# Recurrent stage: squares of the Newton chain on ScalarE, a later row transpose, the last deviations as columns

## The reference

```python
def _L1_ffn_ref(x, ln_w, ln_b, W, b):
    def step(h, _):
        h = h + 0.01 * jnp.tanh(h)
        h = h * jax.nn.sigmoid(h)
        h = _layernorm(h, ln_w, ln_b)
        h = jnp.einsum('bsc,dc->bsd', h, W) + b
        return (h, None)
    x, _ = jax.lax.scan(step, x, None, length=30)
    return x
...
x = x + _L1_ffn_ref(_layernorm(x, axis=-1), ln_w, ln_b, W, b)
```

## Time and profile before

| | us |
|---|---|
| median of 3 runs | 3229.25 (3229.11 to 3229.91) |
| profiled execution, its time | 3229.77 |
| its span, first to last instruction | 3228.0 |
| mean granted TensorE clock | 0.977 of full speed |
| busy: PE, DVE, ACT, POOL | 3034.4, 2831.7, 2382.6, 1722.1 |

### The profile page before, as it was taken

The page is one execution under the profiler, slowest core; times in us unless marked ns, Lnnn a source line. Parts: engine busy times, 40 slices in busy tenths (PEclk is TensorE's granted clock), DMA queues, the critical chain, the costliest instruction groups (busy, mean ns, idle before and its releaser), DMA issues. The chain is left out here.

```text
span 3228.0 us, 67245 instructions
## 1 busy us (share of the span) xinstructions
PE 3034.4 (94%) x16801; PEld 2092.0 (65%) x16801; DVE 2831.7 (88%) x8856; ACT 2382.6 (74%) x4988; POOL 1722.1 (53%) x1101
## 2 busy tenths in 40 slices
PE   6999896999999899999999489999999999999997
PEld 4666665888888577777777355555555555555556
DVE  4777776888888788888888779999999999999997
ACT  4666664444444577777777699999999999999993
POOL 2444444333332121211211058899898888888886
PEclk9999997999999999999999589999999999999999
DMA  4000000000000000000000035555555555555557
GB/s 130 17 19 16 16 16 14 1 0 0 0 0 0 25 14 10 13 12 11 13 10 4 3 132 195 198 184 188 198 190 184 197 195 184 190 199 188 187 197 245
DMA packets 135071, 290.03 MB, mean 90 GB/s; under 512 B 12081, under 2 KB 69601, under 8 KB 135009
## 3 DMA queue, kind: packets, MB, share of 16 engines
q1 hardware_dynamic: 118112, 280.89, 25.7%
q10 hardware_dynamic: 16896, 8.39, 0.9%
HBM read 278.88 MB, written 10.35 MB: 90 GB/s over the span
## 5 line engine op out<-in xcount | busy, mean ns | idle before, releaser
L1077 POOL TENSOR_TENSOR d_g<-d_g,d_rb 128x1024 f32<-128x1024 f32 x480 | 1121.1, 2371 | 269.6 <-DMA d_rb<-d_rstd_rows 269.6
L1265 PE MATMUL d_p_y<-d_g,d_w_main 128*128 128x512 f32 x1856 | 960.9, 599 | 0.0
L1279 PEld LDWEIGHTS d_p_gt<-ident,d_g 128*128 128x128 f32 x3840 | 466.0, 142 | 527.7 <-ACT d_g L1324 365.1
L1142 DVE BATCH_NORM_STATS2 d_stats<-d_p_gt 128x6 f32<-128x256 f32 x1920 | 712.7, 407 | 24.1 <-PE d_p_gt L1279 24.1
L1324 ACT ACTIVATE d_g<-d_th,d_bias 128x512 f32<-128x512 f32 x928 | 670.2, 722 | 67.1 <-DVE d_th L1135 37.3
L1135 DVE SCALAR_TENSOR_TENSOR d_th<-d_th,d_p_y 128x512 f32<-128x512 f32 x960 | 638.0, 665 | 4.4 <-ACT d_th L1320 4.3
L1320 ACT ACTIVATE d_th<-d_p_y,d_bias 128x512 f32<-128x512 f32 x928 | 621.7, 670 | 1.3 <-PE d_p_y L1265 1.2
L1279 PE MATMUL d_p_gt<-ident,d_g 128*128 128x128 f32 x3840 | 592.0, 277 | 0.0
L514 ACT ACTIVATE a_prob<-a_masked,a_neg_max 128x128 f32<-128x128 f32 x1024 | 327.4, 391 | 111.5 <-DVE a_neg_max L334 111.4
L434 PE MATMUL a_p_s<-a_k_heads,a_q_t 128*128 128x512 f32 x768 | 397.4, 599 | 0.5 <-DVE a_k_heads L310 0.5
L451 PEld LDWEIGHTS a_p_pv<-a_v_ones,a_prob_t 128*128 128x128 f32 x3072 | 373.7, 192 | 10.7 <-issue 10.3
(11 more groups left out here) (170 smaller groups left out, 4399.5 us busy)
## 6 DMA issues: line engine op xcount, KB each, us to landing
d_rb<-d_rstd_rows SPq DMA_DIRECT2D x480, 512.0 KB, 5.5
a_adj_in<-in_adj_dram SPq DMA_DIRECT2D x64, 256.0 KB, 2.8
out_dram<-d_out_sb ACTq DMA_DIRECT2D x32, 256.0 KB, 3.3
d_rstd_rows<-d_rstd_row SPq DMA_DIRECT2D x120, 16.0 KB, 1.4
m_w_sb<-in_L_ffn_w_dram SPq DMA_DIRECT2D x2, 512.0 KB
x_sb<-in_x_dram SPq DMA_DIRECT2D x1, 256.0 KB, 2.9
a_w_raw<-in_L_gnn_Wq_dram SPq DMA_DIRECT2D x2, 64.0 KB, 2.1
a_w_raw<-in_L_gnn_Wk_dram SPq DMA_DIRECT2D x2, 64.0 KB, 2.1
```

The lines of the kernel that those rows point to most:

```text
L1077: nc.gpsimd.tensor_tensor(g[:, c, :], g[:, c, :], rb[:, buf, :], ALU.mult).then_inc(s_gs, 1)
L1142: ins = nc.vector.bn_stats(stats[:, q % 2, (j * CT + t) // 2].rearrange("p a s -> p (a s)"), p_gt[:, t * P:(t + 2) * P].rearrange("p (a c) ...
L1265: nc.tensor.matmul(p_y[:, c % 2, cols(u)], w_main[:], g[:, c, cols(u)], start=True, stop=True).then_inc(s_y, 1)
L1279: ins = nc.tensor.transpose(p_gt[:, t * P:(t + 1) * P], g[:, c, t * P:(t + 1) * P], ident[:])
```

## The change: what it does, and the diff

The chain is written so that three of its steps are squares: y^2 after the guess, (v y^2 - 5/3)^2, and (3/8 y)^2. ScalarE makes them (newton_square, with its own places); VectorE keeps six instructions. The chain has 9 steps and ends at the same place as before (r = 3, place 0). The factor -1/2 goes into the weights.

rstd becomes one buffer for each of the four groups, so the guess waits for the row transpose of four groups before. The row transpose moves behind the transposes of unit 0 in slot c mod 4 = 2.

The last four groups' deviations are not transposed, stored, spread and multiplied into g. The last product waits for silu alone, and add_x multiplies by the deviation as a column: four instructions of 128x128 for one of 128x512. It waits for the chain and for s_xb. OUTS becomes 8. Row transposes, copies, SP's loop and GpSimd's loop run over 116 groups (SPREADS) in place of 120. GpSimd's waits for the whole normalised x and for the preparation move ahead of its first multiplication. The preparation has one step more, a memset, and TensorE and ScalarE wait for it.

```diff
-    CHAIN, XCHAIN, PLACES = 10, 12, 3
+    SPREADS = ALL_GROUPS - GROUPS
+    CHAIN, XCHAIN, PREP = 9, 12, 11
-    RSTD_SCALE = 3.0 / 8.0
-    OUTS = 4
+    PLACES = {(0, 0): 0, (0, 1): 1, (1, 0): 3, (1, 2): 5, (2, 2): 7, (3, 0): 8}
+    ACT_PLACES = {(0, 1): 2, (1, 0): 4, (2, 0): 6}
+    CUBIC, SQUARE = 3.0 / 8.0, -1.0 / 2.0
+    OUTS = 8
...
-        rstd = sb("rstd", [P, GTILES])
-        vy2 = sb("vy2", [P, GTILES])
+        rstd = sb("rstd", [P, GROUPS, GTILES])
+        y2 = sb("y2", [P, GTILES])
+        centre = sb("centre", [P, 1])
...
-        v, work, v_x, work_x = (p_nw[:, n * GTILES:(n + 1) * GTILES] for n in range(4))
+        v, vy2, off, v_x, work_x = (p_nw[:, n * GTILES:(n + 1) * GTILES] for n in range(5))
...
# GpSimd
+                pool.wait_ge(s_xn, CHUNKS * UNITS)
+                pool.wait_ge(s_prep, PREP)
                 with pool.Fori(1, CHUNKS + 1) as i:
                     for c in range(CHUNKS):
                         scale(i, c)
-                    pool.wait_ge(s_prep, 10)
-                    pool.wait_ge(s_xn, CHUNKS * UNITS)
...
-                with pool.Fori(CHUNKS + 1, ITERS + 1) as i:
+                with pool.Fori(CHUNKS + 1, ITERS) as i:
...
# VectorE, newton(k, q, n)
-                    y = rstd[:]
+                    y = rstd[:, q, :]
...
-                            wait(dve, s_rt, k)
+                            wait(dve, s_rt, k - GROUPS + 1)
                             ins = nc.vector.tensor_scalar(y.bitcast(I32), v.bitcast(I32), -0.5, MAGIC, ALU.mult, ALU.add)
-                        elif n == 2 or n == 7:
-                            ins = nc.vector.tensor_tensor(work, v, y, ALU.mult)
-                        elif n == 3:
-                            ins = nc.vector.tensor_tensor(vy2[:], work, y, ALU.mult)
-                        elif n == 4:
-                            ins = nc.vector.scalar_tensor_tensor(out=work, in0=vy2[:], scalar=-10.0 / 3.0, in1=work,
+                        elif n == 3 or n == 7:
+                            ins = nc.vector.tensor_tensor(vy2, v, y2[:], ALU.mult)
+                        elif n == 5:
+                            ins = nc.vector.scalar_tensor_tensor(out=y, in0=off, scalar=20.0 / 9.0, in1=y,
                                                                  op0=ALU.add, op1=ALU.mult)
-                        elif n == 5:
-                            ins = nc.vector.tensor_tensor(work, work, y, ALU.mult)
-                        elif n == 8:
-                            ins = nc.vector.scalar_tensor_tensor(out=work, in0=work, scalar=-0.5 * RSTD_SCALE ** 2, in1=y,
-                                                                 op0=ALU.mult, op1=ALU.mult)
                         else:
-                            ins = nc.vector.scalar_tensor_tensor(out=y, in0=work, scalar=5.0 if n == 6 else 1.5, in1=y,
+                            ins = nc.vector.scalar_tensor_tensor(out=y, in0=vy2, scalar=-3.0, in1=y,
                                                                  op0=ALU.add, op1=ALU.mult)
...
# VectorE, add_x(o, u)
+                    n, q = o * UNITS + u, o // GC
                     dve.wait_ge(s_y, units(SLOTS + o, u))
+                    dve.wait_ge(s_nw, CHAIN * (ALL_GROUPS - GROUPS + q + 1))
+                    dve.wait_ge(s_xb, CHUNKS)
                     wait(dve, s_out[n % OUTS], 16 * (n // OUTS))
-                    nc.vector.tensor_tensor(out_sb[:, n % OUTS].rearrange("p (t c) -> p t c", t=UT),
-                                            p_y[:, o % 2, cols(u)].rearrange("p (t c) -> p t c", t=UT),
-                                            x_sb[:, tile:tile + UT, :], ALU.add).then_inc(s_sum, 1)
+                    for t in range(UT):
+                        tile = u * UT + t
+                        ins = nc.vector.scalar_tensor_tensor(
+                            out=out_sb[:, n % OUTS, t * P:(t + 1) * P], in0=p_y[:, o % 2, tile * P:(tile + 1) * P],
+                            scalar=rstd[:, q, o % GC * CT + tile:o % GC * CT + tile + 1], in1=x_sb[:, o * CT + tile, :],
+                            op0=ALU.mult, op1=ALU.add)
+                    ins.then_inc(s_sum, 1)
...
# TensorE, last_product and the row transpose
-                    pe.wait_ge(s_gs, s - CHUNKS + 1)
+                    pe.wait_ge(s_g, units(s - CHUNKS, u))
...
                             if live(s - 2):
                                 transpose_g(s - 2, (c - 2) % CHUNKS, u)
-                        k = GROUPS * i + (c - 9) // GC
-                        if c % GC == 1 and live_group(k):
-                            transpose_rstd(k)
+                            k, q = GROUPS * i + (c - 10) // GC, (c - 10) // GC % GROUPS
+                            if c % GC == 2 and u == 0 and spread_group(k):
+                                transpose_rstd(k, q)
...
# ScalarE
+                def newton_square(k, q, n):
+                    act.wait_ge(s_nw, CHAIN * k + n)
+                    if n == 4:
+                        ins = nc.scalar.activation(off, vy2, ACT.Square, bias=centre[:])
+                    else:
+                        ins = nc.scalar.activation(y2[:], rstd[:, q, :], ACT.Square, scale=1.0 if n == 2 else CUBIC)
+                    ins.then_inc(s_nw, 1)
...
                             nc.scalar.copy(rstd_row[:, q % 2, :], p_rt).then_inc(s_row, 1)
+                        newton_part(i, c, 0)
                         if live(s):
                             tanh(s, c % 2, 1, col)
                             silu(s, c, 0, col)
+                        newton_part(i, c, 1)
...
-                act.wait_ge(s_prep, 7)
+                act.wait_ge(s_prep, PREP)
```

More of the change, by code:

```diff
@@ L1027, in live_group, with spread_group @@
             return not isinstance(k, int) or 0 <= k < ALL_GROUPS
+        def spread_group(k):
+            return not isinstance(k, int) or 0 <= k < SPREADS
         def iterations(eng, body):
@@ L1032, in iterations @@
             body(1)
-            with eng.Fori(2, ITERS) as i:
+            with eng.Fori(2, ITERS - 1) as i:
                 body(i)
+            body(ITERS - 1)
             body(ITERS)
@@ L1062, in _ @@
                 body(0)
-                with sp.Fori(1, ITERS) as i:
+                with sp.Fori(1, ITERS - 1) as i:
                     body(i)
                 for par in range(2):
-                    sp.wait_ge(s_dw[par], 16 * ALL_GROUPS // 2)
+                    sp.wait_ge(s_dw[par], 16 * SPREADS // 2)
                     for j in range(GC):
-                        sp.wait_ge(s_rb[par * GC + j], 16 * ALL_GROUPS // 2)
+                        sp.wait_ge(s_rb[par * GC + j], 16 * SPREADS // 2)
             @block.gpsimd
@@ L1178, in newton_part @@
                     k, q = GROUPS * i + (c - 6) // GC, (c - 6) // GC % GROUPS
[L1179 to L1180 removed]
+                    n = PLACES.get(((c - 6) % GC, place))
+                    if n is not None and live_group(k):
                         newton(k, q, n)
                 def add_x(o, u):
[L1184 removed]
+                    n, q = o * UNITS + u, o // GC
                     dve.wait_ge(s_y, units(SLOTS + o, u))
+                    dve.wait_ge(s_nw, CHAIN * (ALL_GROUPS - GROUPS + q + 1))
+                    dve.wait_ge(s_xb, CHUNKS)
                     wait(dve, s_out[n % OUTS], 16 * (n // OUTS))
[L1187 to L1190 removed]
+                    for t in range(UT):
[5 more added lines that the diff above has]
+                    ins.then_inc(s_sum, 1)
                 def body(i):
@@ L1211, in body @@
                             if c in (0, 1, 4, 5, 8, 9):
-                                for n in range(c % GC * 6, c % GC * 6 + 6):
+                                for n in range(c % GC * 6, min(c % GC * 6 + 6, XCHAIN)):
                                     newton_of_x(1 + c // GC, n)
@@ L1220, in _ @@
                     stats_of_x(GC + c)
-                    for n in range(3 * c, 3 * c + 3):
+                    for n in range(3 * c, min(3 * c + 3, XCHAIN)):
                         newton_of_x(0, n)
@@ L1236, in _ @@
                 link(nc.vector.tensor_copy(bias_bc[:], p_gt[:, P:2 * P]))
+                link(nc.vector.memset(centre[:], -5.0 / 3.0))
                 iterations(dve, body)
-                dve.wait_ge(s_xb, CHUNKS)
                 add_x(CHUNKS - 1, 1)
@@ L1280, in transpose_g, with transpose_rstd @@
                     ins.then_inc(s_gt, 1)
-                def transpose_rstd(k):
+                def transpose_rstd(k, q):
                     pe.wait_ge(s_nw, CHAIN * (k + 1))
                     wait(pe, s_row, k)
-                    nc.tensor.transpose(p_rt, rstd[:], ident[:]).then_inc(s_rt, 1)
+                    nc.tensor.transpose(p_rt, rstd[:, q, :], ident[:]).then_inc(s_rt, 1)
                 def body(i):
@@ L1324, in silu, with newton_part @@
                     nc.scalar.activation(g[:, c, cols(u)], th[:, c % 2, cols(u)], ACT.Silu, bias=col).then_inc(s_g, 1)
+                def newton_square(k, q, n):
```

(8 more changed lines are left out.)

8 lines of the change are left out of this document (2 added, 6 removed).

## The result

| | us |
|---|---|
| before, median | 3229.58 |
| changed kernel, median of 4 runs | 3175.3 (3173.52 to 3179.61) |
| ratio, 95% interval | 0.9836 (0.9821 to 0.9851) |
| changed kernel, profiled execution: its time, its span | 3179.61, 3177.7 |

The change takes 54 us off by the medians; the forecast was 3184 with 3170 to 3207 as range.

What follows compares the result with a forecast made beforehand. The prediction took VectorE, 99.9% busy at 11.07 us a group, as the bound. Its terms gave 3229.8 - 40.1 (chain) + 1.9 (start) - 7 (end) = 3184.6 us, against the median 3184, range 3170 to 3207.

Steps and rivals of the forecast that it cites:

- What bounds the kernel: Iterations 1 to 29 of the recurrent stage: VectorE, 99.9% busy, sets the pace at 11.07 us a group.
- The chain: Recurrent groups: six of ten steps stay on VectorE, three squares go to ScalarE; period 11.07 to 10.72 us, gain 40 us.
- Do the squares make anybody wait: Squares on ScalarE in the recurrent groups: no wait of VectorE on them, the tightest having 0.3 us to spare.
- The row transpose: TensorE, one unit later: its 43.5 us of waits for the chain end, but are worth nothing in time.
- The start: Preparation and iteration 0: memset and waits 0.3 us, eight squares 1.0, GpSimd's later start 0.6; sum +1.9 us.
- The end: Last four groups, without spreads and GpSimd multiplications, with eight output buffers: -7 us, bounds -10 and 0.
- A: Recurrent groups: VectorE, ScalarE and TensorE rub, period 10.80 to 11.0 us, total 3194 to 3216; chance 0.17.
- B: Recurrent groups: ScalarE becomes the bound at 11.41 us with squares of 0.40 us, total about 3263; chance 0.05.
- C: ScalarE: Square shares no table with Tanh and Silu, two loads per square, total some 4150 us; chance 0.03.
- D: Recurrent groups: VectorE alone sets the pace, steps worth more, 10.62 us a group, frictionless end, 3169 to 3176; chance 0.07.
- the forecast's own range: Whole kernel: 3176 to 3196 us, from a period of 10.67 to 10.80 and an end of -3 to -10; chance 0.66.

Runs made afterwards that it cites:

- the version at 10.592: Changed kernel with a chain of eight steps, five on VectorE, epsilon added in two other steps, GpSimd's waits at their old place: 3166.73 us, ratio 0.9806.

## Why the prediction was right, and where its terms were off

**What bounds the kernel.** Right. VectorE was the bound and is the bound; each step on it is worth 0.10 us a group, shown by taking four away (10.673), one more away (10.592, 0.09 us) and adding one (10.775).

**The chain.** Right in direction and in VectorE's 10.67 us; the term was 40 us and measured 45.0. The step that failed is the price of the squares: "Sum 0.48 us, and ScalarE goes to 10.70 us". I took start-to-start distances of small copies and added them, which is right for small instructions in a row; between large activations the neighbours give part of it back, and ScalarE stands at 10.39. So there was no tie between two engines at 10.7, and the 0.05 us a group that I put on top of VectorE's 10.67, 5 of the 115 groups' 45 us, had no cause. The estimate from the Trainium skill, page "ScalarE: Activation LUTs" (ScalarE at 10.67), erred in the same way. The weakness of it was the row: small copies behind one another, and none between large activations.

**Do the squares make anybody wait.** Right: no wait of VectorE for ScalarE in 1230 us.

**The row transpose.** Right that it is worth nothing, by an experiment; also the wait would have gone without it.

**The start.** +1.9 forecast, +3.1 measured. The late start of GpSimd and the clock that came back later make 2.3 us of it, where I had put 0.6: GpSimd's first multiplication began at 1893.67, when the last normalise had ended at 1893.4, and the first product waited 0.69 us for it and then ran at the 1.2 GHz level. Moving the waits back took the 2.3 us off; but the run with four output buffers is rid of 1.9 of them with the late waits in place and the clock back early. So I had left out the clock at the seam between iterations 0 and 1, which has its own price; whether the late waits keep it down isn't shown. The 1.0 us for eight squares was too much, 0.3 to 0.7 by the traces with early waits.

**The end.** -7 forecast, -10.1 measured. My ideal sum, 36.2 us of VectorE's work, was what it took (36.0); "with 2 us for two resources so nearly equal" was the mis-sized part. VectorE at 1.00 did not wait for the DMA engines at 0.87 (3160 to 3165 us). Of the remaining 1.1 us, 0.5 is the last store (2.8 us from the last sum's end to the span's and not 3.3), and 0.4 lies ahead of the first sum, where the chain is shorter. I had counted the gain for the spreads and multiplications that go; but with four output buffers it would have been 1.9 us smaller.

**The rivals.** A (the engines rub) is refuted down to 0.01 us a group, even in the version at 10.592, where TensorE needs 10.49. B needed 0.28 us a square; it is 0.04 to 0.12, and even eight more a group cost only 35 us. C: no table load but the one of the earlier trace rows. D, that VectorE alone sets the pace, is what happened, with the end without friction; its time, 3169 to 3176, holds the measured 3175.3, though not for its reason, that the steps are worth more (10.62 us a group; it was 10.678). I had given it 0.07. So the forecast's own range, 3176 to 3196, was missed by 0.7 us, and the full range held.

**How much was luck.** Between the profiled executions the forecast's 3184.6 is 5.0 us above the 3179.61. Its errors of 4.9 us on the chain and 3.1 on the end have the same sign; the start, 1.2 us the other way, and the stages ahead, which ran 1.75 us longer, took 3 us off them by chance. Against the median 3184 is 8.7 us off.

**The rule** of the Trainium skill, page "ScalarE: Activation LUTs", rules for kernel authors, that multiplications belong on VectorE, would have been the costly way here. The trace disagrees with it as a matter of time: the chain with three steps on ScalarE takes 43 us off (3227.42 to 3184.44), for VectorE is the bound and ScalarE has room. The 9.8% of the run with the squares on VectorE are another matter: four steps with both inputs in SBUF beside a busy GpSimd, one of them no square. That is a price which the prediction missed altogether. Each step of the old chain that takes two tiles has one of them in PSUM, and a square of a tile in SBUF has not. By the count alone three steps would have cost 34 us, an estimate from the price of one step.

**What stays open.** Why a tanh behind a square takes 0.57 us to the next start and behind a silu 0.63 is not explained, only measured. A version with the squares on VectorE and their inputs in PSUM was not tried, so the 34 us are argued, and it isn't shown that nine steps need ScalarE. How the start's cost divides between GpSimd's late waits and the clock is open, too.

## What to carry to other kernels

Where one engine is busy all the time, count its instructions by start-to-start distance, and trust the sum; here engines at 97 to 99% of the bound did not add anything. Before an elementwise step is put on VectorE beside a busy GpSimd, look where both inputs lie: with both in SBUF a step of 0.10 us waited for the rest of GpSimd's instruction, 1.2 us on average. Small activations were cheapest one at a time between large ones. An edit that moves a tile from PSUM to SBUF changes every step that reads it, not only the one it was made for.

## What the runs showed of the hardware that I had not expected

- A 128x32 VectorE instruction costs 0.097 us a group with one input in PSUM and 1.21 us with both in SBUF, GpSimd's instructions being 2.33 us long and GpSimd 92 and 84% busy (2400 to 2600 us); in all 98 groups read it ended with one of GpSimd's.
- A 128x32 activation between a 128x512 silu and a 128x512 tanh costs 0.04 to 0.05 us, a second one beside it 0.11 to 0.12.
- VectorE at 100%, ScalarE at 99% and TensorE at 98% (10.49 of 10.68 us) run in one loop of semaphores without measurable loss; at 10.592 us the loss is 0.01 us a group.
